# Layer statistics and feature tiles in one stage, shared between POOL, ACT and DVE

## The chip, the cores and the metric

The kernel runs on one core of one Trainium2 chip. The metric is the device time of one launch in microseconds (us), the median over runs. The core has five engines that run their own instruction queues and wait for each other through semaphores: PE (TensorE, matmul and transpose), DVE (VectorE), ACT (ScalarE), POOL (GpSimd) and SP (SyncE, which only issues DMAs here).

## The reference

A batch of 16 images and texts goes through a small transformer of four layers on a residual stream h of 16 x 113 tokens (36 image patches and 77 text tokens) of width 256. Each half layer has the form

```
h = tokens(x) ++ txt
h = h + ssm(norm(h));           h = h + moe_top3_of_15(norm(h)) + shared_ffn(norm(h))
h = h + min_gru(norm(h));       h = h + ternary_gelu_ffn(norm(h))
h = h + linear_attention(norm(h));  h = h + bit_glu(norm(h))
h = h + attention(norm(h));     h = h + moe_top1_of_8(norm(h))

def norm(x, eps=1e-5):          # over the 256 features of a token
    m = mean(x); v = mean((x - m)**2)
    return (x - m) / sqrt(v + eps)
```

What matters here is `norm(h)`: per token a mean and a variance, the normalised rows, and these rows transposed (features on partitions) as a float16 high part and a float16 low part, which the matmuls of the next stage read.

## The kernel before

The residual stream `core.h` lies in SBUF as [113 tokens, 16 batches, 256 features], float32. The batches are worked in NG = 4 groups q of GB = 4. `core.xt_hi` and `core.xt_lo` hold the transposed features, [128, KC = 2 chunks, 16 x 113], float16.

The program is a string of stages (`Stage`, line 51, with a `Block` in which each engine has its function). Between two blocks all engines meet, so nothing of a stage starts before the last instruction of the stage ahead. Inside a block each queue runs in the written order. `Chain.step` (line 38) lets an instruction signal and its own engine wait for that signal before the next one. `need` (line 745) is a wait that is left out when its value is zero.

Four places use a pair of stages (lines 2962 to 2975, tags gru, bg, la, mha):

- `stage_norm_stats` (line 586). DVE runs 16 bn_stats (L604: count, mean and squared deviation of the even and of the odd elements of a row, six numbers per token) and then six small operations on 113x16 in `norm_moments` (L616 to L621). ACT has loaded its square root table at the start (L597) and takes the root (L599). DVE takes the reciprocal (L609).
- `stage_features` (line 624). Twice, for two groups: DVE normalises eight batches (L642, 113x256 each), PE transposes each in two chunks into PSUM (L668), ACT copies a group and chunk of 128x452 to the high part (L685), DVE subtracts this from PSUM to get the low part (L656).

`glus`, ahead of the bit_glu stage, and `st0` and `f0`, in the first layer, use the same stage functions and are not touched.

`stage_route` (line 1175, used as m0r and m3r) routes the tokens to experts. It opens with the same work in one stage: DVE makes statistics of eight batches and their moments, ACT the root, DVE the reciprocal, then DVE normalises (L1383, a rotation of XR = 3 buffers `xr`). PE transposes (`turn`, L1271), ACT makes the high parts (L1326), DVE the low parts (L1389), PE the router's logits of the group (`logits`, 24 matmuls). In PE's queue the order is turn 0, turn 1, logits 0, turn 2, logits 1, turn 3, logits 2, logits 3. Beside this the normalised rows go to memory as two float16 halves: ACT makes the high halves (`row_high`, L1321, two buffers `parts`, which it reuses when the DMA of two groups before is done), POOL subtracts to get the low halves (L1248, 113x1024), SP stores them (L1258). The third buffer rule: group 3 is normalised into the buffer of group 0, when POOL is done with that (`row_lo`) and PE has transposed it. POOL makes the constants of the stage first (memsets and iotas, L1229 to L1244), each step waited for. When all logits are there DVE picks the experts (from L1415).

In `stage_bit_gelu` POOL already computes an inverse root as `(variance + eps) ** -0.5`, one value per token at a time (L2135, tile `bgm_rs`).

Of the kernel before, what the change touches and what calls it, by code (L numbers as in the profile page):

```python
# [684 lines left out]
                                act.activation(core.xt_hi[:, c, cols], tp[u][c][:, 0:GT], ACT.Copy).then_inc(hi_done, 1)  # L685


def stage_norm_twice(nc, core, d_row):


# [54 lines left out]
def need(eng, sem, value):  # L745

    if not isinstance(value, int) or value > 0:
        eng.wait_ge(sem, value)
# [426 lines left out]
def stage_route(nc, core, m):  # L1175
# [3 lines left out]


    E, K, N = m.E, m.K, m.blocks
    XR, HB = 3, NB // 2
    with Stage(nc, m.name + "r") as st:
        six = st.sb("six", [L, NB, 6])
        s, dd, var, sd = (st.sb(n, [L, NB]) for n in ("s", "dd", "var", "sd"))
        xr = [st.sb(f"xr{r}", [L, GB, D]) for r in range(XR)]
# [25 lines left out]
        counted, moments, var_ready, sd_ready, rstd_ready = (  # L1212
            st.sem(n) for n in ("counted", "moments", "var_ready", "sd_ready", "rstd_ready"))
        normed, tp_ready, hi_done, lo_done, row_hi, row_lo = (
            st.sem(n) for n in ("normed", "tp_ready", "hi_done", "lo_done", "row_hi", "row_lo"))
# [8 lines left out]
        with nc.Block() as block:  # L1224
            @block.gpsimd
            def _(pool):
                made = Chain(pool, masks)
# [6 lines left out]
                imprecise = dict(allow_small_or_imprecise_dtypes=True)  # L1234
                made.step(pool.iota(iota_e[:], pattern=[[1, E]], base=0, channel_multiplier=0, **imprecise))
                made.step(pool.iota(iota_n[:], pattern=[[1, N]], base=0, channel_multiplier=0, **imprecise))
                made.step(pool.iota(iota_p[:], pattern=[[1, 128]], base=0, channel_multiplier=0, **imprecise))
                made.step(pool.iota(token[:], pattern=[[L, NB]], base=0, channel_multiplier=1, **imprecise))
                made.step(pool.memset(keep[:], 1.0))
# [23 lines left out]
            def _(pe):  # L1263
                def turn(q):
                    u = q % 2

                    need(pe, lo_done, (q - 1) * KC)
                    for j in range(GB):
                        pe.wait_ge(normed, q * GB + j + 1)
# [38 lines left out]

            @block.scalar
            def _(act):  # L1310
                def root(half):
                    g = slice(half * HB, (half + 1) * HB)
                    act.wait_ge(var_ready, half + 1)
                    act.activation(sd[:, g], var[:, g], ACT.Sqrt, bias=core.eps[0:L, :],
                                   scale=1.0 / D).then_inc(sd_ready, 1)

                def row_high(q):
                    act.wait_ge(normed, (q + 1) * GB)
# [10 lines left out]
                act.preload_act_table(ACT.Sqrt)  # L1329
                root(0)  # L1330
                row_high(0)
                high(0)
                row_high(1)
                high(1)
                root(1)
                act.preload_act_table(ACT.Exp)
                row_high(2)
                high(2)
                high(3)
                row_high(3)  # L1340
                act.wait_ge(shifted, 1)
# [10 lines left out]

            @block.vector
            def _(dve):
                def stats(batches):
                    for b in batches:
                        dve.bn_stats(six[:, b, :], core.h[:, b, :]).then_inc(counted, 1)

                def half_moments(half):
                    g = slice(half * HB, (half + 1) * HB)  # L1360
                    me, m2e, mo, m2o = (six[:, g, i] for i in (1, 2, 4, 5))
                    dve.wait_ge(counted, (half + 1) * HB)
                    ch = Chain(dve, moments, half * 4)
                    dve.tensor_tensor(s[:, g], me, mo, ALU.add)
                    ch.step(dve.tensor_tensor(dd[:, g], me, mo, ALU.subtract))
                    ch.step(dve.tensor_tensor(dd[:, g], dd[:, g], dd[:, g], ALU.mult))
                    ch.step(dve.scalar_tensor_tensor(var[:, g], dd[:, g], D / 4.0, m2e, ALU.mult, ALU.add))
                    dve.tensor_tensor(var[:, g], var[:, g], m2o, ALU.add).then_inc(var_ready, 1)
                    ch.step(dve.tensor_scalar(core.mean[:, g], s[:, g], 0.5, None, ALU.mult))

                def invert(half):
                    g = slice(half * HB, (half + 1) * HB)
                    dve.wait_ge(sd_ready, half + 1)
                    dve.reciprocal(core.rstd[:, g], sd[:, g]).then_inc(rstd_ready, 1)
                    dve.wait_ge(rstd_ready, half + 1)

                def normalise(q):

                    need(dve, row_lo, q - XR + 1)
                    need(dve, tp_ready, (q - XR + 1) * KC)  # L1380
                    for j in range(GB):
                        b = q * GB + j
                        dve.tensor_scalar(xr[q % XR][:, j, :], core.h[:, b, :], core.mean[:, b:b + 1],  # L1383
                                          core.rstd[:, b:b + 1], ALU.subtract, ALU.mult).then_inc(normed, 1)
# [7 lines left out]
                stats(range(HB))  # L1392
                half_moments(0)
                stats(range(HB, HB + 2))
                invert(0)
                normalise(0)
                normalise(1)
                stats(range(HB + 2, NB))
                half_moments(1)
                low(0, 0)  # L1400
                low(0, 1)
                invert(1)
                normalise(2)
                low(1, 0)
                normalise(3)
                low(1, 1)
                for q in (2, 3):
                    for c in range(KC):
                        low(q, c)

# [1518 lines left out]
def program(nc, d, out):  # L2929
    Stage.available, Stage.resting = list(nc.free_semaphores), []  # L2930
    with ExitStack() as ctx:
# [155 lines left out]
```

## Time and profile before

| | us |
|---|---|
| runs | 1566.55, 1570.67, 1570.69 (median 1570.67) |
| the profiled execution, its own time | 1579.64 |
| its span | 1577.9 |
| PE, DVE, ACT, POOL busy | 1088.8, 1086.1, 681.2, 456.6 |

The span is from the first to the last instruction that the profiler saw. Busy times are sums over the span; a share says nothing about one stage. In the timeline rows the columns are start, length in us, engine, line, operation, output<-inputs, shapes and count; the idle time before stands in brackets with what ended it. A row with x8 is eight like operations run together: its length is from the start of the first to the end of the last.

### The profile page before, as it was taken

What the parts mean: (1) busy time and instruction counts of PE and PEld (TensorE: products, weight loads), DVE (VectorE), ACT (ScalarE), POOL (GpSimd) and SP (SyncE); (2) the same over time, 40 slices, a digit from 0 to 9 for tenths busy, and PEclk for the clock granted to TensorE, in tenths of its full rate; (3) what the DMA queues carried; (4) which work ended last, traced back from release to release, by engine and by line L of the source; (5) the groups of instructions that cost most, each with busy time, mean ns of one, the idle gap of its engine ahead of it and who ended that gap; (6) DMA issues with size and microseconds to landing.
All of it is one profiled execution on the core that took longest, in us unless ns stands there. A gap on an engine that the chain in (4) does not pass through costs nothing. (4 is left out here: it accounts for less than half of the span.)

```text
span 1577.9 us, 31368 instructions
## 1 busy us (share of the span) xinstructions
PE 1088.8 (69%) x9744; PEld 779.6 (49%) x9744; DVE 1086.1 (69%) x2356; ACT 681.2 (43%) x1360; POOL 456.6 (29%) x607
## 2 busy tenths in 40 slices
PE   4515887774299997675767868266488786469991
PEld 2212232224288883453545745144376665458881
DVE  3867999997555555547967754888667776746653
ACT  4505555553265453114426622244266655234440
POOL 0051777772254545610001100000033333222203
PEclk9557999995599998887968977688556766579996
DMA  6600000001345544202000000000012222112213
GB/s 198 206 4 11 0 1 0 1 1 48 94 123 137 159 129 144 79 29 80 1 0 1 1 1 0 0 1 0 28 58 105 82 82 82 48 40 67 62 52 117
DMA packets 45459, 89.64 MB, mean 57 GB/s; under 512 B 8096, under 2 KB 34373, under 8 KB 42437
## 3 DMA queue, kind: packets, MB, share of 16 engines
q1 hardware_dynamic: 38274, 67.97, 13.7%
q0 software_dynamic: 6912, 18.88, 4.3%
q8 instruction: 83, 1.36, 0.4%
q10 hardware_dynamic: 144, 1.05, 0.2%
q14 instruction: 46, 0.38, 0.1%
HBM read 71.84 MB, written 16.04 MB: 56 GB/s over the span
## 5 line engine op out<-in xcount | busy, mean ns | idle before, releaser
L909 POOL TENSOR_TENSOR scan_ch<-scan_hs,scan_ct 128x452 f32<-128x452 f32 x128 | 143.4, 1141 | 81.4 <-DVE scan_hs L1019 67.3
L932 PE MATMUL scan_py<-scan_ch,ident 128*128 128x452 f32 x256 | 130.8, 600 | 41.1 <-POOL scan_ch L909 31.0
L1019 DVE TENSOR_TENSOR_SCAN scan_hs<-scan_abar,scan_bx 128x452 f32<-128x452 f32 x128 | 132.9, 1079 | 0.8 <-ACT scan_abar L981 0.5
L2620 POOL TENSOR_TENSOR mha_prob_lo<-mha_prob,mha_prob_hi 113x452 f16<-113x452 f32 x64 | 65.3, 1042 | 135.2 <-ACT mha_prob_hi L2781 135.2
L458 PE MATMUL m0x_ph<-m0x_xb,m_w_hi 128*128 128x128 f16 x456 | 100.0, 221 | 0.7 <-ACT m0x_xb L1625 0.5
L459 PE MATMUL m0x_ph<-m0x_xb,m_w_hi 128*128 128x128 f16 x456 | 100.0, 221 | 0.0
L460 PE MATMUL m0x_ph<-m0x_xb,m_w_lo 128*128 128x128 f16 x456 | 99.6, 220 | 0.0
L1690 DVE TENSOR_SCALAR m3x_a<-m3x_ph,m3x_b 128x128 f32<-128x128 f32 x184 | 49.7, 344 | 69.2 <-ACT m3x_ah L1651 67.3
L932 PEld LDWEIGHTS scan_py<-scan_ch,ident 128*128 128x128 f32 x256 | 40.5, 192 | 112.4 <-POOL scan_ch L909 104.6
L981 ACT ACTIVATE scan_abar<-ssm_dt,ssm_a 128x448 f32<-128x448 f32 x128 | 80.8, 638 | 23.7 <-DVE scan_hs L1019 22.1
L1687 DVE SCALAR_TENSOR_TENSOR m0x_a<-m0x_ph,m0x_b,m0x_gate 128x128 f32<-128x128 f32 x114 | 34.7, 347 | 72.1 <-issue 36.3
L1651 ACT ACTIVATE m3x_ah<-m3x_ph,m3x_b 128x128 f16<-128x128 f32 x184 | 50.0, 382 | 65.4 <-PE m3x_ph L460 61.4
L458 PE MATMUL m3x_ph<-m3x_xb,m_w_hi 128*128 128x128 f16 x368 | 74.6, 225 | 3.2 <-DVE m3x_al L1701 2.9
L459 PE MATMUL m3x_ph<-m3x_xb,m_w_hi 128*128 128x128 f16 x368 | 74.6, 225 | 0.0
L460 PE MATMUL m3x_ph<-m3x_xb,m_w_lo 128*128 128x128 f16 x368 | 74.4, 224 | 0.0
L1011 DVE TENSOR_TENSOR scan_bx<-scan_pb,ssm_dx 128x452 f32<-128x452 f32 x128 | 72.9, 610 | 0.4 <-PE scan_pb L919 0.4
L2613 POOL MEMSET mha_v_hi<- 113x768 f16 x1 | 0.7, 737 | 241.3 <-POOLq L635 241.3
L1536 POOL DMA_INDIRECT m0x_xg<-m_rows,m0x_idx x57 | 55.5, 974 | 44.4 <-POOL m0x_idx L1534 41.8
L1772 POOL DMA_INDIRECT shared_got<-m_out,m_slot x48 | 51.3, 1069 | 36.5 <-issue 26.9
L976 ACT ACTIVATE scan_ct<-scan_pc 128x452 f32<-128x452 f32 x64 | 35.0, 547 | 60.1 <-POOL scan_ch L909 41.5
L1635 ACT ACTIVATE m0x_gate<-m0x_ph,m0x_b 128x128 f32<-128x128 f32 x114 | 35.6, 363 | 35.8 <-PE m0x_ph L460 27.2
L458 PE MATMUL m3x_py<-m_w_hi,m3x_ah 128*128 x184 | 50.1, 272 | 1.2 <-DVE m3x_yo L1708 0.8
(675 smaller groups left out, 3888.1 us busy)
## 6 DMA issues: line engine op xcount, KB each, us to landing
mha_wbuf<-m3w SPq DMA_DIRECT2D x16, 1024.0 KB, 4.8
tok_wbuf<-m0w SPq DMA_DIRECT2D x15, 768.0 KB, 5.5
m0x_b<-m0b SPq DMA_DIRECT2D x57, 128.0 KB
m_out<-m0x_yo SPq DMA_DIRECT2D x57, 128.0 KB
m3x_b<-m3b SPq DMA_DIRECT2D x23, 128.0 KB, 3.0
m_out<-m3x_yo SPq DMA_DIRECT2D x23, 128.0 KB
m_rows<-m0r_parts SPq DMA_DIRECT2D x4, 448.0 KB
m_rows<-m3r_parts SPq DMA_DIRECT2D x4, 448.0 KB
```

Of the source, the lines that this page charges most:

```text
L458: pe.matmul(out, w_hi, x_hi, start=start, stop=False)
L459: pe.matmul(out, w_hi, x_lo, start=False, stop=False)
L460: return pe.matmul(out, w_lo, x_hi, start=False, stop=stop)
L909: pool.tensor_tensor(ch[r][:], hs[r][:], ct[n % 2][:], ALU.mult).then_inc(weighed, 1)
L932: pe.matmul(py[c][:, 0:GT], core.ident[:], ch[u % R][:], start=n == 0, stop=n == NS - 1).then_inc(summed, 1)
L981: act.activation(abar[c][:, 0:GT].rearrange("p (b t) -> p b t", t=L)[:, :, 1:L], ssm.dt[:, c, cols].rearrange("p (b t) -> p b t", t=L)[:, ...
L1011: dve.tensor_tensor(bx[u % R][:], pb[n % 2][:, 0:GT], ssm.dx[:, c, cols], ALU.mult).then_inc(drive, 1)
L1019: dve.tensor_tensor_scan(hs[u % R][:], abar[c][:, 0:GT], bx[u % R][:], 0.0, ALU.mult, ALU.add).then_inc(scanned, 1)
L1536: pool.indirect_dma_start(xg[p][:], None, m.rows[:, :], bass.IndirectOffsetOnAxis(ap=idx[p][:, 0:1], axis=0)).then_inc(gathered[p], 16)
L1651: ins = act.activation(a_hi[r][:, f, :], ph[p][:, f, :], ACT.Relu, bias=b1[p][:, 0, f:f + 1])
L1772: pool.indirect_dma_start(self.got[j][k][:], None, m.out[:, :], bass.IndirectOffsetOnAxis(ap=m.slot[:, b, k:k + 1], axis=0)).then_inc(self ...
L2620: pool.tensor_tensor(prob_lo[g][:], prob[g % 2][:], prob_hi[g][:], ALU.subtract).then_inc(p_low, 1)
```

## The change

The class `RowNorm` holds the statistics of a stage, and `stage_norm_features` replaces both stages of a pair; `stage_route` uses the same class.

- `stats(dve, q)`: DVE's bn_stats of the four batches of group q.
- `moments(pool, q)`: ten POOL operations on 113x4 make `rstd = (variance + eps) ** -0.5` and `shift = -mean * rstd`. Seven of them are waited for by POOL itself. A signal `scaled` closes the group.
- `normalise(eng, q)`: `x * rstd + shift`. Group 0 is done by DVE (tensor_scalar), groups 1 to 3 by ACT (Identity with `scale` and `bias` taken from one column each).
- The orders in the new stage: DVE stats 0, stats 1, normalise 0, stats 2, stats 3, then the low parts of groups 0 to 3; ACT normalise 1, high 0, normalise 2, high 1, normalise 3, high 2, high 3; POOL moments 0 to 3; PE the transposes of groups 0 to 3. `xr` has three buffers instead of two.
- In `stage_route` DVE has the same order. POOL makes moments 0 and 1 ahead of its constants, moments 2 behind the third of them, moments 3 behind the four iotas. ACT no longer loads the square root table; its order is normalise 1, row_high 0, high 0, normalise 2, row_high 1, high 1, normalise 3, high 2, row_high 2, high 3, row_high 3, and normalise 3 waits for POOL's first `row_lo`.

```diff
+class RowNorm:
+    BY_VECTOR = 0
+    STEPS = 7
...
+    def begin(self, pool):
+        pool.memset(self.half[:], -0.5).then_inc(self.half_set, 1)
+    def stats(self, dve, q):
+        for b in range(q * GB, (q + 1) * GB):
+            dve.bn_stats(self.six[:, b, :], self.core.h[:, b, :]).then_inc(self.counted, 1)
+    def moments(self, pool, q):
...
+        pool.wait_ge(self.counted, (q + 1) * GB)
+        ch = Chain(pool, self.chain, q * self.STEPS)
+        pool.tensor_tensor(var, m2e, m2o, ALU.add)
+        pool.tensor_tensor(s, me, mo, ALU.add)
+        ch.step(pool.tensor_tensor(dd, me, mo, ALU.subtract))
+        pool.tensor_scalar(nmean, s, -0.5, None, ALU.mult)
+        ch.step(pool.tensor_tensor(dd, dd, dd, ALU.mult))
+        ch.step(pool.tensor_scalar(dd, dd, D / 4.0, None, ALU.mult))
+        ch.step(pool.tensor_tensor(var, var, dd, ALU.add))
+        ch.step(pool.tensor_scalar(var, var, 1.0 / D, EPS, ALU.mult, ALU.add))
+        ch.step(pool.tensor_tensor(rstd, var, self.half[:, g], ALU.pow))
+        ch.step(pool.tensor_tensor(self.shift[:, g], nmean, rstd, ALU.mult))
+        pool.sem_inc(self.scaled, 1)
+    def normalise(self, eng, q):
+        eng.wait_ge(self.scaled, q + 1)
+        for j in range(GB):
...
+            if q == self.BY_VECTOR:
+                eng.tensor_scalar(out, x, rstd, shift, ALU.mult, ALU.add).then_inc(self.by_vector, 1)
+            else:
+                eng.activation(out, x, ACT.Identity, bias=shift, scale=rstd).then_inc(self.by_scalar, 1)
...
+def stage_norm_features(nc, core, name):
...
+            def _(pool):
+                norm.begin(pool)
+                for q in range(NG):
+                    norm.moments(pool, q)
...
+                norm.normalise(act, 1)
+                high(0)
+                norm.normalise(act, 2)
+                high(1)
+                act.wait_ge(tp_ready, KC)
+                norm.normalise(act, 3)
+                high(2)
+                high(3)
...
+                norm.stats(dve, 0)
+                norm.stats(dve, 1)
+                norm.normalise(dve, 0)
+                norm.stats(dve, 2)
+                norm.stats(dve, 3)
+                for q in range(NG):
+                    low(q)
...
 @@ stage_route, block.scalar
+                def normalise(q):
+                    need(act, row_lo, q - XR + 1)
+                    need(act, tp_ready, (q - XR + 1) * KC)
+                    norm.normalise(act, q)
...
-            stage_norm_stats(nc, core, tag + "s", core.h)
-            stage_features(nc, core, tag + "f", core.h)
+            stage_norm_features(nc, core, tag + "f")
             stage()
...
-            stage_norm_stats(nc, core, "mhas", core.h)
-            stage_features(nc, core, "mhaf", core.h)
+            stage_norm_features(nc, core, "mhaf")
```

## Rows read from the trace of the kernel before

**Rows 1.** The page: busy time of the engines, and the chain that ended last.
```profile
PE 1088.8 (69%) x9744; PEld 779.6 (49%) x9744; DVE 1086.1 (69%) x2356; ACT 681.2 (43%) x1360; POOL 456.6 (29%) x607
...
POOL m3c_got L1772 1%; DMA m3c_got<-m_out,m_slot 0%; DVE h L1781 0%; DVEq L1797 0%; POOLq L78 0%; POOLq L35 0%; POOLq L1524 0%
```

**Rows 2.** Stretches: length, busy PE, PEld, DVE, ACT, POOL; granted clock; DMA share, GB/s.
```profile
799.02:817.26 18.24, 6.49 (x32) 5.85 (x32) 16.39 (x47) 5.50 (x10) 0.00 (x0) 0.61 0.00 0
...
358.86:386.84 27.98, 16.14 (x128) 15.31 (x128) 20.90 (x54) 10.85 (x16) 10.94 (x21) 0.51 0.17 51
```

**Rows 3.** Timeline of the bg pair and the start of the stage behind.
```profile
799.02 5.32 DVE L604 BATCH_NORM_STATS2 bgs_six<-h 113x6 f32<-113x256 f32 x16 [0.32 <-PEq L1965]
...
806.56 2.68 DVE L642 TENSOR_SCALAR bgf_xr<-h,mean,rstd 113x256 f32<-113x256 f32 x8 [0.55 <-DVE rstd L609]
...
815.52 0.98 ACT L685 ACTIVATE xt_hi<-bgf_tp 128x452 f16<-128x452 f32 x2 [0.52 <-PE bgf_tp L668]
...
817.59 0.65 PE L2148 MATMUL bgm_ph<-bg_wq,xt_hi 128*113 128x512 f16 x1 [1.91 <-PEq L635]
```

**Rows 4.** POOL's prices: two tiles (ns min/median/max), page group, timeline of three stages.
```profile
L1545 POOL COPY m0x_b<-m_b x57: 186/188/1282, 425.3 to 591.8; 128x4 f32 x57
...
L2135 POOL TENSOR_TENSOR bgm_rs<-bgm_mv,bgm_half x16: 547/862/865, 824.2 to 890.0; 113x1 f32<-113x1 f32 x16
...
L909 POOL TENSOR_TENSOR scan_ch<-scan_hs,scan_ct 128x452 f32<-128x452 f32 x128 | 143.4, 1141 | 81.4 <-DVE scan_hs L1019 67.3
...
425.34 0.19 POOL L1545 COPY m0x_b<-m_b 128x4 f32 x1
425.47 0.18 POOL L1534 COPY m0x_idx<-m_ids 128x1 uint32<-128x1 uint32 x1
...
359.52 0.29 POOL L1232 TENSOR_SCALAR_AFFINE_SELECT m0r_below<-m0r_below 113x113 f16<-113x113 f16 x1
359.88 0.17 POOL L1235 IOTA m0r_iota_e<- 113x15 f32 x1
...
360.89 0.30 POOL L1239 MEMSET m0r_keep<- 113x240 f32 x1
...
361.68 0.31 POOL L1244 MEMSET m0r_place<- 1x10 f32 x6
...
725.86 1.22 POOL L425 TENSOR_SCALAR_AFFINE_SELECT gru_heads<-gru_heads 128x16 f16<-128x16 f16 x4
```

**Rows 5.** Timeline: DVE and POOL at the same time, in bgm and in m0r.
```profile
843.55 0.62 DVE L2227 TENSOR_TENSOR bgm_a_lo<-bgm_full,bgm_a_hi 128x452 f16<-128x452 f32 x1
...
843.71 0.86 POOL L2135 TENSOR_TENSOR bgm_rs<-bgm_mv,bgm_half 113x1 f32<-113x1 f32 x1 [5.74 <-DVE bgm_mv L2215]
...
366.04 4.21 POOL L1248 TENSOR_TENSOR m0r_parts<-m0r_xr,m0r_parts 113x1024 f16<-113x1024 f32 x2 [4.05 <-ACT m0r_parts L1321]
...
366.07 2.05 DVE L1357 BATCH_NORM_STATS2 m0r_six<-h 113x6 f32<-113x256 f32 x6
368.15 2.12 DVE L1364 TENSOR_TENSOR m0r_s<-m0r_six 113x8 f32<-113x8 f32 x1
```

**Rows 6.** ACT's prices: tiles (ns min/median/max) and the group of the bg pair.
```profile
L2193 ACT ACTIVATE bgm_full<-bgm_pt,bg_lnb,bg_lnw x32: 710/717/728, 836.6 to 902.9; 128x452 f32<-128x452 f32 x32
...
L685 ACT ACTIVATE xt_hi<-bgf_tp 128x452 f16<-128x452 f32 x8 | 3.9, 545 | 6.8 <-PE bgf_tp L668 6.8
...
L1646 ACT ACTIVATE m0x_ah<-m0x_a x57: 412/416/418, 433.0 to 597.5; 128x256 f16<-128x256 f32 x57
```

**Rows 7.** The m0r opening: DMA in 40 slices of 355 to 400, PE, DVE.
```profile
GB/s 0 0 0 0 7 0 0 0 0 0 0 0 127 262 193 235 5 0 0 0 111 270 30 15 0 0 0 0 157 247 8 0 0 0 0 0 0 0 0 7
...
378.00 0.26 PE L458 MATMUL m0r_plog<-m_router_hi,xt_hi 128*113 128x15 f16 x1 [1.58 <-DVE xt_lo L1389]
...
380.37 1.75 PE L1271 MATMUL m0r_tp<-ident,m0r_xr 113*128 113x113 f32 x8
...
386.84 0.41 DVE L1415 TENSOR_REDUCE m0r_top<-m0r_plog 113x16 f32<-113x240 f32 x1 [3.13 <-PE m0r_plog L460]
```

More of the change, by code:

```diff
@@ L685, in _, with __init__, wait_rows @@
                                 act.activation(core.xt_hi[:, c, cols], tp[u][c][:, 0:GT], ACT.Copy).then_inc(hi_done, 1)
+class RowNorm:
+    BY_VECTOR = 0
+    STEPS = 7
+    def __init__(self, st, core, rows):
+        self.core, self.rows = core, rows
+        self.six = st.sb("six", [L, NB, 6])
+        self.sum, self.diff, self.var, self.nmean, self.rstd, self.shift, self.half = (
+            st.sb(n, [L, NB]) for n in ("sum", "diff", "var", "nmean", "rstd", "shift", "half"))
+        self.xr = [st.sb(f"xr{r}", [L, GB, D]) for r in range(rows)]
+        self.half_set, self.counted, self.chain, self.scaled = (
+            st.sem(n) for n in ("half_set", "counted", "moments", "scaled"))
+        self.by_vector, self.by_scalar = st.sem("by_vector"), st.sem("by_scalar")
+    def begin(self, pool):
[4 more added lines that the diff above has]
+    def moments(self, pool, q):
+        g = slice(q * GB, (q + 1) * GB)
+        me, m2e, mo, m2o = (self.six[:, g, i] for i in (1, 2, 4, 5))
+        s, dd, var, nmean, rstd = (t[:, g] for t in (self.sum, self.diff, self.var, self.nmean, self.rstd))
+        if q == 0:
+            pool.wait_ge(self.half_set, 1)
+        pool.wait_ge(self.counted, (q + 1) * GB)
[14 more added lines that the diff above has]
+        for j in range(GB):
+            b = q * GB + j
+            out, x, rstd, shift = self.xr[q % self.rows][:, j, :], self.core.h[:, b, :], self.rstd[:, b:b + 1], self.shift[:, b:b + 1]
+            if q == self.BY_VECTOR:
+                eng.tensor_scalar(out, x, rstd, shift, ALU.mult, ALU.add).then_inc(self.by_vector, 1)
+            else:
+                eng.activation(out, x, ACT.Identity, bias=shift, scale=rstd).then_inc(self.by_scalar, 1)
+    def wait_rows(self, eng, q, j):
+        if q == self.BY_VECTOR:
+            eng.wait_ge(self.by_vector, j + 1)
+        else:
+            eng.wait_ge(self.by_scalar, (q - 1) * GB + j + 1)
@@ new lines, in stage_norm_features, with _, high, low @@
+def stage_norm_features(nc, core, name):
+    with Stage(nc, name) as st:
+        norm = RowNorm(st, core, 3)
+        tp = [[st.ps(f"tp{u}{c}", [128, 512]) for c in range(KC)] for u in range(2)]
+        tp_ready, hi_done, lo_done = st.sem("tp_ready"), st.sem("hi_done"), st.sem("lo_done")
+        with nc.Block() as block:
+            @block.gpsimd
+            def _(pool):
+                norm.begin(pool)
+                for q in range(NG):
+                    norm.moments(pool, q)
+            @block.tensor
+            def _(pe):
+                for q in range(NG):
+                    need(pe, lo_done, (q - 1) * KC)
+                    for j in range(GB):
+                        norm.wait_rows(pe, q, j)
+                        for c in range(KC):
+                            last = pe.transpose(tp[q % 2][c][:, j * L:(j + 1) * L],
+                                                norm.xr[q % 3][:, j, c * 128:(c + 1) * 128], core.ident[0:L, 0:L])
+                            if j == GB - 1:
+                                last.then_inc(tp_ready, 1)
+            @block.scalar
+            def _(act):
+                def high(q):
+                    for c in range(KC):
+                        act.wait_ge(tp_ready, q * KC + c + 1)
+                        act.activation(core.xt_hi[:, c, q * GT:(q + 1) * GT], tp[q % 2][c][:, 0:GT],
+                                       ACT.Copy).then_inc(hi_done, 1)
+                norm.normalise(act, 1)
[6 more added lines that the diff above has]
+                high(3)
+            @block.vector
+            def _(dve):
+                def low(q):
+                    for c in range(KC):
+                        cols = slice(q * GT, (q + 1) * GT)
+                        dve.wait_ge(hi_done, q * KC + c + 1)
+                        dve.tensor_tensor(core.xt_lo[:, c, cols], tp[q % 2][c][:, 0:GT], core.xt_hi[:, c, cols],
+                                          ALU.subtract).then_inc(lo_done, 1)
+                norm.stats(dve, 0)
[3 more added lines that the diff above has]
+                norm.stats(dve, 3)
+                for q in range(NG):
+                    low(q)
@@ L1181, in stage_route @@
     E, K, N = m.E, m.K, m.blocks
-    XR, HB = 3, NB // 2
+    XR = 3
     with Stage(nc, m.name + "r") as st:
-        six = st.sb("six", [L, NB, 6])
-        s, dd, var, sd = (st.sb(n, [L, NB]) for n in ("s", "dd", "var", "sd"))
-        xr = [st.sb(f"xr{r}", [L, GB, D]) for r in range(XR)]
+        norm = RowNorm(st, core, XR)
+        xr = norm.xr
         parts = [st.sb(f"parts{u}", [L, GB, 2, D], F16) for u in range(2)]
@@ L1210, in stage_route @@
         pids = st.ps("pids", [128, N])
[L1212 to L1215, printed above, removed]
+        tp_ready, hi_done, lo_done, row_hi, row_lo = (
+            st.sem(n) for n in ("tp_ready", "hi_done", "lo_done", "row_hi", "row_lo"))
         stored = [st.sem(f"stored{u}") for u in range(2)]
@@ L1226, in _ @@
             def _(pool):
+                norm.begin(pool)
+                norm.moments(pool, 0)
+                norm.moments(pool, 1)
                 made = Chain(pool, masks)
@@ L1234, in _ @@
                 imprecise = dict(allow_small_or_imprecise_dtypes=True)
+                norm.moments(pool, 2)
                 made.step(pool.iota(iota_e[:], pattern=[[1, E]], base=0, channel_multiplier=0, **imprecise))
@@ L1238, in _ @@
                 made.step(pool.iota(token[:], pattern=[[L, NB]], base=0, channel_multiplier=1, **imprecise))
+                norm.moments(pool, 3)
                 made.step(pool.memset(keep[:], 1.0))
@@ L1268, in turn @@
                     for j in range(GB):
-                        pe.wait_ge(normed, q * GB + j + 1)
+                        norm.wait_rows(pe, q, j)
                         for c in range(KC):
@@ L1310, in _ @@
             def _(act):
[L1311 to L1315, printed above, removed]
+                def normalise(q):
+                    need(act, row_lo, q - XR + 1)
+                    need(act, tp_ready, (q - XR + 1) * KC)
+                    norm.normalise(act, q)
                 def row_high(q):
-                    act.wait_ge(normed, (q + 1) * GB)
+                    norm.wait_rows(act, q, GB - 1)
                     need(act, stored[q % 2], q // 2 * (16 * len(ROWS)))
@@ L1327, in high @@
                                        ACT.Copy).then_inc(hi_done, 1)
-                act.preload_act_table(ACT.Sqrt)
-                root(0)
+                act.preload_act_table(ACT.Exp)
+                normalise(1)
                 row_high(0)
                 high(0)
+                normalise(2)
                 row_high(1)
                 high(1)
-                root(1)
-                act.preload_act_table(ACT.Exp)
+                normalise(3)
+                high(2)
                 row_high(2)
-                high(2)
                 high(3)
@@ L1354, in _ @@
             def _(dve):
[L1355 to L1384, printed above, removed]
                 def low(q, c):
@@ L1390, in low @@
                                       ALU.subtract).then_inc(lo_done, 1)
[L1392 to L1407, printed above, removed]
+                norm.stats(dve, 0)
+                norm.stats(dve, 1)
+                norm.normalise(dve, 0)
+                norm.stats(dve, 2)
+                norm.stats(dve, 3)
+                for q in range(NG):
                     for c in range(KC):
```

## The prediction

> **What bounds the kernel now.** I read the page first: PE and DVE are each busy 69% of the span, and the chain of waits covers only the last per cent (the combine stage), so neither tells what one stage is worth [rows 1]. The kernel is a string of stages with a barrier between them. So each changed stage has to be read as its own small race, and its length carries to the end one for one. There are six: four pairs "statistics, then features" (before the gru, bg, la and mha stages) and the opening of the two routing stages. The table of stretches shows the bg pair 18.24 us long (the other three repeat it, within 0.2), and the first routing opening, from its first bn_stats to the first reduction of the logits, 27.98 (the second one repeats it, within 0.1) [rows 2]. In a pair DVE is busy 16.3 of 18.2 us and POOL not at all: DVE is the bound, ACT has two thirds of its time free.
>
> The timeline of the bg pair [rows 3] shows how: 16 bn_stats in 5.32 us (a pitch of 0.327), moments, root and reciprocal until 806.5, then two rounds of eight normalisations on DVE (2.68, so 0.33 each), each followed by transposes, high copies on ACT and low parts on DVE. The last low part ends at 817.26, the next stage's first matmul starts 0.33 later, and that gap stays.
>
> **The change, part by part.** Let t = 0 be the start of the first bn_stats, and M the time that POOL needs for one group's moments.
>
> *POOL's moments.* Per group ten instructions on 113x4 elements: three that nothing waits for, seven that are each waited for, one of them pow. The trace has a POOL copy of 128x4 at 0.186, and its two-input 128x452 product at 1.141, so (1.141-0.186)/452 = 2.1 ns an element: four elements cost nothing, and any of these operations but pow is about 0.19 [rows 4]. Two POOL operations without a wait between them start 0.13 apart (425.34 and 425.47). With a wait on the previous one the gap is 0.07 (359.52+0.29 to 359.88) or 0.14 (four selects of 0.198 in 1.22 us are 0.34 apart) [rows 4]. Pow on 113x1 takes 0.547 when undisturbed. So M = 3 x 0.13 + 6 x (0.19+0.07) + (0.55+0.07) = 2.57, plus what three more elements of pow cost (3e), plus about 0.05 for the final signal. The trace has no pow wider than one element. Its bounds: e = 0.002 (the slope of the product) to e = 0.36 (all that pow costs over a copy). I take e = 0.05, because at this width the other POOL operations of the trace are start-up nearly alone; that gives M = 2.8. With both ends and the two gaps, M lies between 2.5 and 4.1.
>
> *What DVE's normalisation does to it.* While POOL makes group 1, DVE normalises group 0. The rows show that the two lock each other out: DVE's tiny 113x8 sum took 2.12, up to the end of POOL's second 113x1024 subtraction (366.04+4.21), and POOL's pow took 0.86 instead of 0.55 while DVE's two-input operation ran [rows 5]. POOL lost 0.31 to 0.62 us of DVE work, so four normalisations of 0.33 may cost it 4 x 0.33 = 1.3 at most and nothing at least; I take d = 0.5, once per stage. bn_stats is not slowed: six of them beside POOL's first subtraction took 2.05, the usual pitch.
> The Trainium skill ("SBUF — State Buffer", Who interferes with whom) speaks against the change here: it says that the pair of ports is an exclusive lock held for a whole instruction, and that tensor_scalar in its two-port mode takes it. The rows agree that one fully blocks the other; by the letter of that rule d would be 1.3 and each stage 0.8 longer than in my sum.
>
> *ACT's normalisation.* ACT has no operation of just this form in the trace. Identity with both pointer operands on 128x452 takes 0.717, the plain copy 0.545, so the two operands cost 0.17; a plain copy of 128x256 takes 0.416 [rows 6]. So 0.59 each, and as ACT's operations overlap by 0.11 (two of 0.545 in 0.98, rows 3), a pitch of 0.49: 1.97 per group against 1.33 on DVE. Bounds 0.42 to 0.72 each.
>
> *The pair as one stage.* Group q's moments are ready at S(q) = 1.46 + (q+1)M, with d added from q = 1: the first four bn_stats end at 3 x 0.327 + 0.41, and later ones are never late (groups 2 and 3 are counted by 8.5). Two chains then end the stage:
> - ACT's: from S(1), three groups of normalisation and four of high copies (0.89 each), 3 x 1.97 + 4 x 0.89, then starts and the last low part, 0.85: 10.3. End = 11.8 + 2M + d.
> - POOL's: from S(3), one normalisation 1.97, two pairs of high copies 1.87, the last low part and waits 0.75: 4.6. End = 6.05 + 4M + d.
> At M = 2.8, d = 0.5 they give 17.9 and 17.75. So a pair goes from 18.2 to 17.9: 0.3 gained, 1.2 in all four. The removed work (half of DVE's normalisation, the stage boundary inside the pair, the root's table load, which lay beside bn_stats) is thus nearly all given back: POOL's chain and ACT's queue are late next. PE's transposes (8 in 1.75 us [rows 7], two to a batch) keep up with batches that come every 0.49. The table load that goes costs nothing now, and the one of the next stage stays.
>
> *The routing stages.* The same start, but POOL's queue holds more: three mask operations behind moments(1) (0.36 for the select and, as an estimate, 0.47 for two memsets), four iotas behind moments(2) (359.88 to 360.89), memsets behind moments(3) (to 361.99, 1.1) [rows 4], and only then the first low-row subtraction (2.1), which before ran from 7.2 [rows 5]. ACT's normalise(3) waits for it, as it frees the third buffer, and everything behind it in ACT's queue waits too. S(1) = 7.6, S(2) = 11.2, S(3) = 15.1, the subtraction from 16.1 to 18.2. Then ACT: normalise(3) to 20.3, high(2) to 21.2; row_high(2), now ahead of high(3), needs the first group stored. The DMA traffic shows 448 KB stored 3.0 us after its subtraction ended (slices of 1.125 us: 127 and 262 GB/s from 368.5) [rows 7]: 21.2, so it costs no further wait, and ends at 22.2; high(3) 23.1, last low part 23.8. PE: logits(2), 2.37 each (378.00 to 380.37), from 21.9 to 24.3, logits(3) to 26.7; reduction at 26.8 instead of 27.98 [rows 7]. Gain 1.2 each, 2.4 in both, moving by 4 us per us of M. The old stage lost more to order than this one: turn(3) sat behind logits(1) until 380.37, and logits(3) ran after logits(2) [rows 7]. The later low-row subtractions are hidden behind the long selection work on DVE and may stall it by at most one of 2.1.
>
> **Sum.** -1.2 - 2.4 = -3.6. The profiled execution took 1579.64 (span 1577.9), 9 us more than the median of the runs; the stages are timed in it, and I carry the difference over to the median: 1570.67 - 3.6 = 1567.1. Not in the sum: the granted clock. In these stretches it averages 0.61 and 0.51 of full speed, so most of them lies at the 1.2 GHz level [rows 2], and so may the first matmuls of the stage behind; a rise that moves by 1 us moves a stage by half of that, as an estimate 2 us in all, either way.
>
> **The rivals.**
> - *Pow pays per element (the slower side).* Place: POOL's chain, four times a stage. If e = 0.36, M = 3.7 to 3.8; a pair ends at 6.05 + 15.2 + 0.5 = 21.7, 3.5 longer each; a routing opening is 4 us later than in my sum, 2.8 longer than before. 14 + 5.6 = +19.6: 1590. It decides from M = 2.9 on, where the pairs stop gaining. For it: 0.36 us for one element is much for a start-up cost. Against it: nothing in the trace. The Trainium skill ("GPSIMD Engine Reference", Instruction dispatch) calls the inner loop an ordinary software loop per element, which would make this rival the rule.
> - *Gaps and locks at their upper end.* Waits at 0.14 and d = 1.3 make M = 3.2: pairs +2.0 each, routing +1.2 each, +10: 1581. For it the selects' pitch of 0.34; against it the 0.07 of the mask chain, in a stage that is itself changed.
> - *All at the lower end.* M = 2.5, d = 0.2: ACT's chain sets the pairs, 17.0 (-1.2 each), routing -2.7 each, -10: 1561.
> - *The change doesn't remove DVE's bound* (Identity needs a table load, or the merged stage's boundary costs as much): under 3 us, inside the ranges.
>
> **How the numbers follow.** My forecast's case, M from 2.6 to 3.0, 50% (1562 to 1571 is its own range); pow per element 27%; gaps and locks 8%; all low 15%. A measurement here can tell about 0.3%, 4.7 us. Faster by more: the low case and four tenths of mine, 35%. Slower by more: the two slow ones and a little of mine, 37%. The rest, 28%, is no change. The range reaches from the low case to pow at full price: 1560 to 1590.
>
> **What would show it.** Pow on 113x4 between 0.55 and 0.7 (forecast) or about 1.6 (first rival). M as the distance of two pow in a pair, 2.8. ACT's normalisation at 0.59 with a pitch of 0.49. The pairs at 17.9, ACT hardly idle after S(1); if ACT waits for POOL before group 3, M is over 2.9. In routing, ACT's wait for the first low-row subtraction until about 18.2, and the reduction at 26.8. I am wrong if pow is over 0.8, if DVE's normalisation stretches beyond 2.5 us or stalls POOL by over 1 us, or if a wait appears that I don't name.

## The result and the profile after

The changed kernel takes 1581.87 us (median of 4 runs, 1580.36 to 1585.24) beside 1570.68 of the kernel before on the same chip: ratio 1.0081, 95% interval 1.0056 to 1.0105, so 11.2 us slower (8.8 to 16.5). The forecast of 1567.1 and its sign were wrong; the time lies inside the range of 1560 to 1590.

The page of the kernel after, busy times and chain, to be read beside [rows 1]:

```profile
PE 1103.1 (70%) x9744; PEld 777.7 (49%) x9744; DVE 1046.2 (66%) x2228; ACT 706.1 (45%) x1418; POOL 523.2 (33%) x853
...
DMA m3c_got<-m_out,m_slot 1%; POOL m3c_got L1861 0%; DVE h L1870 0%; POOLq L78 0%; POOLq L1886 0%; POOLq L35 0%; POOLq L1613 0%
```

DVE has 40 us less to do, ACT 25 and POOL 67 more, and the kernel is slower: as before, neither total nor chain tells what a stage is worth. The stretches do, with the columns of [rows 2]: the bg pair, now one stage, and the first routing opening.

```profile
794.39:814.54 20.15, 7.93 (x32) 4.82 (x32) 11.30 (x28) 9.68 (x20) 11.24 (x41) 0.54 0.00 1
357.53:386.79 29.26, 17.45 (x128) 14.66 (x128) 11.43 (x28) 14.93 (x25) 21.95 (x62) 0.53 0.15 43
```

All four pairs take 20.15 to 20.19 (before 18.0 to 18.3), the two openings 29.3 and 28.9 (before 28.0 and 27.9). The six stretches sum to 138.9 against 128.5: +10.3, which is the measured 11.2 within its interval. The two profiled executions are only 3.4 apart (1583.07 and 1579.64), because that of before spent 319.6 us from the first opening's end to the gru pair where that of after spent 309.5, in work that the change doesn't touch. That stretch takes 309 to 311 us in seven of the thirteen profiles of this study and 318 to 324 in the other six, with the old and the changed routing stage on both sides; that is why the changed stretches are compared and not the spans.

The timeline of the bg pair after (columns as in [rows 3]) shows what sets the 20.15:

```profile
794.39 2.71 DVE L711 BATCH_NORM_STATS2 bgf_six<-h 113x6 f32<-113x256 f32 x8 [0.32 <-PEq L2054]
...
799.30 1.44 DVE L741 TENSOR_SCALAR bgf_xr<-h,bgf_rstd,bgf_shift 113x256 f32<-113x256 f32 x4 [2.20 <-POOLq L732]
...
802.87 2.08 ACT L743 ACTIVATE bgf_xr<-h,bgf_shift,bgf_rstd 113x256 f32<-113x256 f32 x4 [19.18 <-POOLq L732]
802.96 0.20 POOL L722 TENSOR_TENSOR bgf_var<-bgf_six 113x4 f32<-113x4 f32 x1 [0.18 <-POOL bgf_shift L731]
...
804.34 0.20 POOL L728 TENSOR_TENSOR bgf_var<-bgf_var,bgf_diff 113x4 f32<-113x4 f32 x1
804.62 0.19 POOL L729 TENSOR_SCALAR bgf_var<-bgf_var 113x4 f32<-113x4 f32 x1
804.90 1.04 POOL L730 TENSOR_TENSOR bgf_rstd<-bgf_var,bgf_half 113x4 f32<-113x4 f32 x1
806.02 0.20 POOL L731 TENSOR_TENSOR bgf_shift<-bgf_nmean,bgf_rstd 113x4 f32<-113x4 f32 x1
806.30 2.08 ACT L743 ACTIVATE bgf_xr<-h,bgf_shift,bgf_rstd 113x256 f32<-113x256 f32 x4 [0.50 <-POOLq L732]
806.39 0.20 POOL L722 TENSOR_TENSOR bgf_var<-bgf_six 113x4 f32<-113x4 f32 x1 [0.18 <-POOL bgf_shift L731]
...
809.79 2.08 ACT L743 ACTIVATE bgf_xr<-h,bgf_shift,bgf_rstd 113x256 f32<-113x256 f32 x4 [0.56 <-POOLq L732]
...
812.33 2.23 DVE L804 TENSOR_TENSOR xt_lo<-bgf_tp,xt_hi 128x452 f16<-128x452 f32 x4 [2.33 <-ACT xt_hi L786]
814.89 0.65 PE L2237 MATMUL bgm_ph<-bg_wq,xt_hi 128*113 128x512 f16 x1 [2.33 <-PEq L761]
```

POOL works through from 795.95 to 809.65, four groups at 3.43 to 3.57 each (802.96 to 806.39 for the third). ACT waits for POOL before each of its three groups, the last two times 0.50 and 0.56. The last group's scale comes 15.4 after the first bn_stats, and the fixed tail behind it, 4.75, ends the stage. One pow is 1.04 of the 3.43.

### The profile page after: what moved, and what is told of

Read it like the earlier page. It is cut to its first block and busy times, and to the rows that moved or that the text cites. A ratio compares the mean times of both kernels' runs of the same rounds, so it can differ in the third digit from the quotient of the medians.

```text
span 1581.0 us, 31516 instructions
## 1 busy us (share of the span) xinstructions
PE 1103.1 (70%) x9744; PEld 777.7 (49%) x9744; DVE 1046.2 (66%) x2228; ACT 706.1 (45%) x1418; POOL 523.2 (33%) x853
## 5 line engine op out<-in xcount | busy, mean ns | idle before, releaser
L458 PE MATMUL m3x_ph<-m3x_xb,m_w_hi 128*128 128x128 f16 x368 | 74.1, 223 | 2.5 <-DVE m3x_al L1790 2.5
L459 PE MATMUL m3x_ph<-m3x_xb,m_w_hi 128*128 128x128 f16 x368 | 74.1, 224 | 0.0
```

What stands on the lines that cost most here:

```text
L458: pe.matmul(out, w_hi, x_hi, start=start, stop=False)
L459: pe.matmul(out, w_hi, x_lo, start=False, stop=False)
```

## The experiments

Each run is compared with the kernel before on its own chip; the chips differ by up to 1%, so only ratios are compared. "Stretches" is the sum of the four pairs and two openings in the run's profile, less the 128.5 of before.

```
                 pairs          openings      stretches  ratio to before [95%]
after            20.15..20.19   29.3, 28.9    +10.3      1.0081 [1.0056, 1.0105]
e1_no_pow        17.21..17.29   25.9, 25.6     -8.0      0.9953 [0.9929, 0.9978]
e2_pairs_only    20.22..20.53   28.0, 27.9     +8.7      1.0063 [1.0042, 1.0083]
e3_route_only    18.03..18.28   29.3, 29.0     +2.5      1.0003 [0.9981, 1.0025]
e4_halves        18.95..19.23   25.6, 25.5     -1.3      0.9962 [0.9941, 0.9984]
e5_dve_two       20.43..20.67   28.0, 27.9     +9.4      1.0071 [1.0050, 1.0093]
e7_dve_halves    15.47..15.55   28.0, 27.9    -10.5      0.9909 [0.9879, 0.9938]
e8_both          15.31..15.61   25.6, 25.5    -15.5      0.9894 [0.9855, 0.9934]
e9_dve_all       15.47..15.51   25.7, 25.6    -15.3      0.9867 [0.9829, 0.9906]
e10_no_lock      15.47..15.52   25.8, 25.7    -15.1      0.9862 [0.9803, 0.9921]
e11_no_lock2     15.49..15.53   23.2, 23.0    -20.3      0.9841 [0.9796, 0.9886]
```

### e1: the same kernel without pow

```diff
-        pool.memset(self.half[:], -0.5).then_inc(self.half_set, 1)
+        pool.memset(self.half[:], 1.0).then_inc(self.half_set, 1)
...
-        ch.step(pool.tensor_scalar(var, var, 1.0 / D, EPS, ALU.mult, ALU.add))
-        ch.step(pool.tensor_tensor(rstd, var, self.half[:, g], ALU.pow))
+        ch.step(pool.tensor_scalar(var, var, 1e-9, 0.01, ALU.mult, ALU.add))
+        ch.step(pool.tensor_tensor(rstd, var, self.half[:, g], ALU.mult))
```

The kernel leaves out the inverse root; the number of instructions and their shapes stay.

> The changed kernel with pow taken out of POOL's moments: a product stands in its place, so the inverse root is not computed and rstd is a constant near 0.01. Ten POOL operations remain per group. Theory (POOL's chain of moments ends the pairs, pow is 0.84 of its 3.44 us): the distance of two groups falls to 2.6, each pair from 20.2 to about 17.2 (there ACT's queue takes over), each routing opening by 3.4 from 29.3 and 28.9; the whole about 8 us under the kernel before. Rival (ACT's queue is the bound): the pairs stay near 20. Rival (locks with DVE): the distance of groups 0 and 1 stays over 3.

Measured: 0.9953 (0.9929 to 0.9978), 7.4 us under before, pairs 17.25, openings 25.9 and 25.6. In the bg pair the multiplication that stands for pow, and two of ACT's groups:

```profile
L730 POOL TENSOR_TENSOR bgf_rstd<-bgf_var,bgf_half x4: 200/200/203, 796.6 to 804.5; 113x4 f32<-113x4 f32 x4
...
801.85 0.95 ACT L786 ACTIVATE xt_hi<-bgf_tp 128x452 f16<-128x452 f32 x2
802.71 2.07 ACT L743 ACTIVATE bgf_xr<-h,bgf_shift,bgf_rstd 113x256 f32<-113x256 f32 x4
```

0.84 us less per group turns 20.2 into 17.3, and ACT's second group starts without a wait in brackets: with M near 2.6 (801.91 to 804.52 between two of these multiplications) ACT's chain ends the stage, as the formula says (11.8 + 2 x 2.6 + 0.1 = 17.1). The stretches fell by 18.3 against after. So what is worth 18 us here is one instruction, 24 times.

### e2 and e3: each half of the change alone

```diff
 e2: stage_route as in the kernel before
 e3: all four pairs as in the kernel before
```

> The four pairs as changed, the routing stage as before. Theory: four times 18.2 to 20.2, so 8 us slower than before. Rival (the time is lost in the routing stages by the late low-row subtraction): no slower than before.

> The routing stage as changed, the four pairs as before. Theory: the two openings are 1.3 and 0.9 longer, so about 2 us slower than before, inside 0.3%. Rival (routing is where it is lost): 8 us or more slower.

The pairs alone cost 0.6% (0.4 to 0.8), the routing stages alone nothing that can be told (0.9981 to 1.0025), with stretches of +8.7 and +2.5. Together +11.2, against +10.3 for both: the parts add up within 1 us. Most of the loss is in the pairs.

### e6: pow and the product by width

Fourteen operations, each waited for, were added to the stage that makes the constants; everything else is the kernel before.

```diff
+                for op in (ALU.pow, ALU.mult):
+                    for n in (1, 2, 4, 8, 16, 32, 64):
+                        ch.step(pool.tensor_tensor(wide[2][0:L, 0:n], wide[0][0:L, 0:n], wide[1][0:L, 0:n], op))
```

> The kernel before with 14 more POOL operations in its first stage, on 113 partitions and 1, 2, 4, 8, 16, 32 and 64 elements: pow, then a product, each waited for. Theory: pow costs 0.163 us per element over a start of 0.38: 0.55, 0.71, 1.04, 1.69, 3.0, 5.6, 10.8; the product stays at 0.2 up to 16. Rival (a step between 1 and 4 that doesn't go on, as of a loop that fills): 16 elements under 1.5. The gap behind a waited operation should show as 0.07 to 0.09.

The profile's rows for this line in four short windows, so that each holds two neighbouring widths (the outer two of the three numbers, in ns, are the two operations), and two groups of all by form, where pow and product of a width are together:

```profile
L486 POOL TENSOR_TENSOR const_wide<-const_wide x2: 571/637/703, 2.5 to 3.2; 113x1 f32<-113x1 f32 x1, 113x2 f32<-113x2 f32 x1
...
L486 POOL TENSOR_TENSOR const_wide<-const_wide x2: 1017/1326/1635, 4.0 to 5.0; 113x4 f32<-113x4 f32 x1, 113x8 f32<-113x8 f32 x1
...
L486 POOL TENSOR_TENSOR const_wide<-const_wide x2: 1635/2266/2898, 5.0 to 6.8; 113x8 f32<-113x8 f32 x1, 113x16 f32<-113x16 f32 x1
...
L486 POOL TENSOR_TENSOR const_wide<-const_wide x2: 5426/7986/10547, 9.7 to 15.2; 113x32 f32<-113x32 f32 x1, 113x64 f32<-113x64 f32 x1
...
L486 POOL TENSOR_TENSOR const_wide<-const_wide 113x64 f32<-113x64 f32 x2 | 10.9, 5432 | 0.2
...
L486 POOL TENSOR_TENSOR const_wide<-const_wide 113x4 f32<-113x4 f32 x2 | 1.2, 609 | 0.2
```

Pow takes 0.571, 0.703, 1.017, 1.635, 2.898, 5.426 and 10.547 at widths 1, 2, 4, 8, 16, 32 and 64: a start of 0.4 and 0.16 per element, on a straight line, so the rival's step (16 elements under 1.5) isn't there. The product takes 2 x 0.609 - 1.017 = 0.201 at width 4 and 2 x 5.432 - 10.547 = 0.317 at 64: 2 ns per element, the slope that [rows 4] gave. The slope of one operation said nothing of the other's: they are a factor of 80 apart.

### e4: half as many calls of POOL's moments, twice as wide

```diff
-        g = slice(q * GB, (q + 1) * GB)
+        g = slice(q * 2 * GB, (q + 1) * 2 * GB)
...
-                norm.normalise(dve, 0)
                 norm.stats(dve, 2)
                 norm.stats(dve, 3)
+                norm.normalise(dve, 0)
```

> The changed kernel with POOL's moments in two calls of eight batches in place of four of four; DVE makes all statistics first, then normalises group 0. Theory (the fixed part of ten operations is paid four times, pow per element either way): a call costs 3.44 + 4 x 0.163 = 4.1, both are done at 11.0 where four took 15.3; ACT's queue ends the pair at about 17.3, a gain of 0.9 on the pair of before; the routing openings fall to about 25. In all 10 us under the kernel before. Rival (pow's cost grows faster with width, or ACT starting later costs it all): pairs at 18.2 or more.

The kernel gains 0.4% (0.2 to 0.6), so a part of the loss was the fixed cost of ten instructions, seven of them waited for, paid four times. The openings came out at 25.6 and 25.5 (about 25 expected). But the pairs took 19.0 where 17.3 were expected; that is the rival's side, for another reason than its two. Of its bg pair (first bn_stats at 787.06), pow and the row that ACT waits for:

```profile
L730 POOL TENSOR_TENSOR bgf_rstd<-bgf_var,bgf_half x2: 1670/1672/1673, 791.9 to 796.4; 113x8 f32<-113x8 f32 x2
...
798.45 2.08 ACT L743 ACTIVATE bgf_xr<-h,bgf_shift,bgf_rstd 113x256 f32<-113x256 f32 x4 [1.38 <-POOLq L732]
```

Pow at 1.67 is again 0.16 per element more. The second call ends 11.4 after the start, and from there ACT still has two normalisations and three pairs of high copies in its queue, in this order: 11.4 + 7.6 = 19.0. I had not counted that high 1 stands behind normalise 2, which waits for POOL.

### e5: DVE normalises group 2 as well

```diff
-    BY_VECTOR = 0
+    BY_VECTOR = (0, 2)
```

In DVE's queue normalise 2 stands behind the low part of group 0, in ACT's it is gone. The routing stage is that of before.

> The pairs as changed, but DVE normalises groups 0 and 2 and ACT only 1 and 3; the routing stage as before. Theory (POOL's chain is the bound): group 3 is ready no sooner, the pairs stay at 20.2 and the time is that of the kernel with the pairs alone changed, 8 over before. Rival (ACT's queue of twelve normalisations is the bound): 1.9 less in each pair, so the time of before.

The pairs took 20.4 to 20.7, nothing gained: with the work shared out in another way the stage still ends at POOL's last group. ACT's busy time fell to 7.6 a pair, from 9.7, and bought nothing.

### e7: no POOL in the pairs

One stage per pair as in the change, but DVE makes the moments, for eight batches at a time, ACT the root, DVE the reciprocal and the shift; DVE normalises groups 0 and 2, ACT 1 and 3, and each group has its own PSUM tiles. The routing stage is that of before.

```diff
+                norm.stats(dve, range(8))
+                norm.moments(dve, 0)
+                norm.stats(dve, range(8, 10))
+                norm.invert(dve, 0)
+                norm.normalise(dve, 0)
+                norm.stats(dve, range(10, 16))
+                norm.moments(dve, 1)
+                low(0, 0)
+                norm.invert(dve, 1)
+                norm.normalise(dve, 2)
```

> One stage for each pair without POOL: DVE makes the moments by halves of eight batches, ACT the root, DVE the reciprocal and the shift; DVE normalises groups 0 and 2, ACT 1 and 3; eight PSUM tiles so that PE never waits for the low parts; the routing stage as before. Theory (what made the change slow is only where the moments are made; merging the stages and sharing the normalisation is sound): the pair ends at about 14.3 where it took 18.2, 15 us in all under before. Rival (sharing with ACT gains nothing in any form): pairs at 17.5 or more.

0.9909 (0.9879 to 0.9938), pairs 15.5. The bg pair as a stretch:

```profile
784.62:800.12 15.50, 6.55 (x32) 5.79 (x32) 14.91 (x48) 9.71 (x19) 0.00 (x0) 0.61 0.00 0
```

The merged stage, ACT's share of the normalisation and the separate PSUM tiles are thus together worth 2.7 us per pair once the moments are off POOL; no run parts the three. The pair is 1.2 longer than the 14.3 expected. DVE is busy 14.9 of 15.5: it is the bound again.

### e8 and e9: the routing stage

e8 is e7's pairs with e4's routing stage. e9 takes DVE's moments into the routing stage too, and POOL keeps its constants and the low rows.

> Pairs of e7_dve_halves (DVE makes the moments of eight batches at a time, ACT the root, DVE and ACT two groups of normalisation each) together with the routing stage of e4_halves (POOL's moments in two calls). Theory: the six stretches are separate stages and add up. Pairs 15.5 each (-2.7 against before, -10.9 in all), routing openings 25.5 each (-2.45, -4.9 in both), sum of the six 128.5 -> 113; kernel -15.5, ratio 0.990. Rival (the stages are not separate: the granted clock or a later stage takes back what an earlier one gains): the stretches come out as in the two runs but the ratio stays at that of e7 alone, 0.991 or above 0.993.

> As e8_both, and the routing stages too leave the moments to DVE by halves with ACT's root, DVE normalises groups 0 and 2, ACT 1 and 3, POOL keeps only its constants and the low rows; ACT makes the high rows of groups 2 and 3 last. Theory (the routing opening is bound by when the normalised groups come, and behind that by PE): group 0 and 1 can be normalised from 4.8 after the first bn_stats instead of 6.9, groups 2 and 3 from 10.9 instead of 12; PE's turns and logits then run without long waits from 10.4: 22 per opening (20 to 23.6 by PE's clock), -6 each against before; sum of the six about 106, ratio 0.985. Rival (PE's logits and the row path set the opening anyway): opening stays at 25 to 25.6, ratio as e8_both, 0.990.

e8's stretches add up to the -15.5 expected, and its ratio is 0.9894 (0.9855 to 0.9934); the interval also holds the 0.991 of the rival, so only the stretches decide. e9's openings stayed at 25.7 where 22 were expected, the number of its rival. Its m0r timeline, DVE and POOL:

```profile
366.05 2.12 POOL L1430 TENSOR_TENSOR m0r_parts<-m0r_xr,m0r_parts 113x1024 f16<-113x1024 f32 x1 [4.80 <-ACT m0r_parts L1503]
366.33 1.87 DVE L779 TENSOR_TENSOR m0r_sum<-m0r_six 113x8 f32<-113x8 f32 x1
...
370.25 2.12 POOL L1430 TENSOR_TENSOR m0r_parts<-m0r_xr,m0r_parts 113x1024 f16<-113x1024 f32 x1 [2.08 <-ACT m0r_parts L1503]
370.32 2.08 DVE L797 TENSOR_TENSOR m0r_shift<-m0r_nmean,m0r_rstd 113x8 f32<-113x8 f32 x1
```

Two operations that take 0.17 alone stood still until POOL's subtraction ended (368.17 and 372.37), as [rows 5] shows for the kernel before: 3.6 us of DVE's chain.

### e10 and e11: the long subtractions moved out of the way

```diff
 e10, from e9:
-    XR = 3
+    XR = 4
+                pool.wait_ge(norm.scaled, 4)
                 for q in range(NG):
                     pool.wait_ge(row_hi, q + 1)
 e11, from e10:
-                pool.wait_ge(norm.scaled, 4)
+                pool.wait_ge(norm.by_vector, 2 * GB)
```

> As e9_dve_all, but in the routing stages POOL begins its four low-row subtractions only when DVE has made the last shift, and a fourth buffer of normalised rows takes away ACT's wait for the first of them. Theory (in e9 DVE's small sum of 1.87 and its shift of 2.08 us stood still for the rest of POOL's 113x1024 subtraction, 1.7 + 1.9 us, and that ate the gain of the earlier moments): both are back at 0.17, groups 2 and 3 can be normalised from 10.5 after the first bn_stats instead of 14.4, and PE is the bound from there: openings 23.6 instead of 25.7 (22.8 to 24.4), -2 each; kernel -4 against e9, ratio to before about 0.984. Rival (PE's 96 logits matmuls at the granted clock and its turns set the opening, wherever the moments are): 25 to 25.7 and the ratio of e9, 0.987.

> As e10_no_lock, but POOL begins its low-row subtractions only when DVE has also normalised group 2. Theory (in e10 the small moments were free, 0.17 each, but the same subtractions then held DVE's four normalisations of group 2, 5.10 instead of 1.38): the normalisation is back at 1.4, POOL's two subtractions lie beside low parts, which read PSUM and were not held in e4 (1.17 for two); turn 2 ends some 3.5 earlier, and PE is the bound: openings 22.8 to 24.4, -2 each against e10; ratio about 0.983. Rival (PE and its granted clock set the opening): 25 to 25.7 and the ratio of e10.

e10's small operations were back at 0.17, and its openings still took 25.8 and 25.7, so its expectation failed as well. DVE and POOL from the timeline of e10's m0r:

```profile
368.10 5.10 DVE L805 TENSOR_SCALAR m0r_xr<-h,m0r_rstd,m0r_shift 113x256 f32<-113x256 f32 x4
368.15 4.25 POOL L1431 TENSOR_TENSOR m0r_parts<-m0r_xr,m0r_parts 113x1024 f16<-113x1024 f32 x2 [7.61 <-DVE m0r_shift L797]
```

The subtractions now held DVE's four normalisations, 5.10 for 1.38. The rival (PE sets the opening) would fit e10 as well; e11 tells them apart. Its m0r, timeline and stretch:

```profile
368.74 1.38 DVE L805 TENSOR_SCALAR m0r_xr<-h,m0r_rstd,m0r_shift 113x256 f32<-113x256 f32 x4
...
370.21 4.21 POOL L1431 TENSOR_TENSOR m0r_parts<-m0r_xr,m0r_parts 113x1024 f16<-113x1024 f32 x2 [9.04 <-DVE m0r_xr L805]
...
373.01 1.16 DVE L1543 TENSOR_TENSOR xt_lo<-m0r_tp,xt_hi 128x452 f16<-128x452 f32 x2 [1.82 <-ACT xt_hi L1509]
...
358.03:381.20 23.17, 15.89 (x128) 15.41 (x128) 15.02 (x49) 14.66 (x24) 9.40 (x21) 0.52 0.14 41
```

The openings fell to 23.2 and 23.0, and the low part beside the subtraction took its usual 1.16 for two. e11 has the lowest ratio of this study, 0.9841 (0.9796 to 0.9886) of before: 1545.47 us beside 1571.39. Its interval overlaps with those of e9 and e10; that it is better than they are rests on the stretches.

In e4, e7 and e9 to e11 the ratios stand for 4 to 7 us more than the six stretches explain (e11: -25.0 against -20.3). The interval of e4 doesn't hold its stretches (-6.0, from -9.2 to -2.5, against -1.3), those of the others do. In e7 to e11 a part may lie in the gru stage behind its pair, 73.1 to 74.1 us beside 74.6 before and 77.8 and 77.5 in e3 and e6; the rest stays open.

## Why the prediction was wrong, point by point

- **The step that failed is "POOL's moments", M = 2.8; it is 3.43.** The structure of the sum held: with the measured M and lock, POOL's chain gives 6.05 + 4 x 3.43 + 0.14 = 19.9 for a pair (measured 20.2: the last scale comes 0.1 later and the tail behind it is 4.75, not 4.6), and the opening, 26.8 and 4 us per us of M, gives 29.3, or 28.9 with the smaller lock (29.3 and 28.9). Against before that is 4 x 1.7 for the pairs and 2 x 1.0 to 1.4 for the openings, +8.8 to +9.6 where the sum had -3.6, against +10.3 in the stretches.
- **Half of the 0.66 is pow.** I took e = 0.05 per further element, "because at this width the other POOL operations of the trace are start-up nearly alone". It is (1.037 - 0.547)/3 = 0.163, and e6 shows the line over 64 widths. The bounds of 0.002 and 0.36 held it; the choice between them rested on operations of another kind. The only row of this operation, 0.547 where a copy takes 0.186, could not part start from slope; e6 does: of the 0.36 over the copy 0.16 is the element and 0.2 a longer start. The first rival had the right mechanism and the right sign, at 0.36 twice too dear: hence 1590 for a kernel at 1582. With its gap pow takes 1.12 where my sum had 0.77.
- **The other half, 0.31, is small change.** Waited steps are 0.28 to 0.31 apart and not 0.26 (804.34, 804.62, 804.90), as the operations take 0.20 to 0.23 and the gap is 0.08; the pitch without a wait is 0.15 to 0.19 and not 0.13; with the signal behind it the last step is 0.37 (806.02 to 806.39), 0.09 over an ordinary one where I had 0.05. Each of these terms was a little low. Either half alone makes M = 3.1 and a pair 6.05 + 12.4 + 0.1 = 18.6: already slower than 18.2. I wrote that the case decides from M = 2.9 on, and forecast 0.1 away from it.
- **The second rival's 1581 is luck.** It has nearly the measured time and, at 6.05 + 4 x 3.2 + 1.3 = 20.15, even the measured pair, but from waits of 0.14 and a lock of 1.3 where the trace has 0.08 and 0.14, and with no price for pow.
- **The lock, d = 0.5: 0.14.** Group 1, beside DVE's normalisation, took 3.57 between two pow (797.90 to 801.47), the later groups 3.43. DVE's four took 1.44. The letter of the rule (1.3) was far off here: in those 1.44 us POOL's short operations took 0.20 to 0.26 in place of 0.20 to 0.23, so it seems that they slip between DVE's four. With long ones on POOL's side it holds in full, as e9 and e10 show. The Trainium skill ("SBUF — State Buffer", Who interferes with whom) also says that a DVE instruction with at most one SBUF input outside the two-port modes doesn't contend; e11's low parts, which read one operand from PSUM, agree (1.16 for two).
- **ACT's normalisation, 0.59 at a pitch of 0.49: held**, 0.587 and 0.50 (four in 2.08):

```profile
L743 ACT ACTIVATE bgf_xr<-h,bgf_shift,bgf_rstd x12: 584/587/601, 802.9 to 811.3; 113x256 f32<-113x256 f32 x12
L730 POOL TENSOR_TENSOR bgf_rstd<-bgf_var,bgf_half x4: 1036/1037/1042, 797.9 to 808.3; 113x4 f32<-113x4 f32 x4
```

- **Two chains in the pair: held.** After has POOL's, e1 ACT's, each where the formula puts the change-over. That there is something to gain behind the two chains held as well: 2.7 a pair without POOL's (e7, where ACT keeps the root and PSUM has more tiles).
- **Routing: order right, the openings 2.5 and 2.1 late.** Of m0r after, POOL's first subtractions and what ACT waits for:

```profile
375.89 4.20 POOL L1378 TENSOR_TENSOR m0r_parts<-m0r_xr,m0r_parts 113x1024 f16<-113x1024 f32 x2
378.04 2.08 ACT L743 ACTIVATE m0r_xr<-h,m0r_shift,m0r_rstd 113x256 f32<-113x256 f32 x4 [3.86 <-POOL m0r_parts L1378]
...
381.43 1.06 ACT L1451 ACTIVATE m0r_parts<-m0r_xr 113x1024 f16<-113x1024 f32 x1 [0.45 <-DMA m_rows<-m0r_parts]
```

The first subtraction ends 20.5 after the start where I had 18.2, and ACT waits 3.86 for it, as forecast. The store that I had cost-free adds 0.45.
- **Small slips in the working**, none of which moves the outcome: 3 x 0.327 + 0.41 is 1.39, the 1.46 has a start in it that isn't named (POOL began at 1.56); by its own terms M is 2.6 at the low end, not 2.5; and DVE's busy time in the pair is 16.39, not 16.3.
- **The clock (2 us either way): no effect of the change is shown.** The pair's granted clock is 0.54 against 0.61 in [rows 2], and the gru stage behind its pair took 77.9, at 0.82, for 74.6, at 0.86. But e3 and e6, whose pairs are those of before, took 77.8 and 77.5 in that stage, at 0.82 as well, so it doesn't take the change to get there. Each is one execution, and the sum of the stretches alone comes within 1 us of the measured difference.

## What to carry to other kernels

A chain of tiny operations on one engine costs its steps, and its elements only where one of them has a price per element, as pow here: before you move it to a slower engine, multiply the whole chain, wait gaps and signals too, by the number of groups, and forecast a change of place only if the sum stands with every term at its upper row. One row at width one can't part start from slope; time an operation that costs three times its neighbours there at the width you mean to use, or keep the dear end as the forecast. And a long POOL operation belongs beside DVE work that reads PSUM or makes bn_stats, not beside SBUF-to-SBUF steps on the critical path: starting the subtractions 1.4 us later was worth 2.6 us per opening (e10 to e11).

## What the runs showed of the hardware

- Pow on POOL is 0.4 us and 0.16 us per element of each partition, from 1 to 64 elements; a product on the same shapes is 0.2 and 0.002. The Trainium skill ("GPSIMD Engine Reference", Instruction dispatch) speaks of an ordinary loop per element, for a two-input operation and without naming pow; the runs agree, with prices that lie a factor of 80 apart.
- What the lock between DVE and POOL costs differs with the length of the other engine's operation: four DVE operations of 0.4 cost a queue of POOL's 0.2 us operations 0.14 us together, while one POOL operation of 2.1 held a DVE operation of 0.17 for up to 1.9, and two of them (4.25 together beside their usual 4.2) held four DVE normalisations for 3.7 (e10).
